# Two conditioned attention layers: VectorE's transpose for the next first film moves behind the keys' reciprocal

## The reference

```
# layer 0
xn = layer_norm(x) * w + b;  q, k, v = xn @ Wq + bq, xn @ Wk + bk, xn @ Wv + bv
y  = softmax_over_keys(q k^T + mask) v                  # per head, 256 x 256 scores
h  = (layer_norm(y) * w2 + b2) * (1 + scale) + shift
x  = x + silu(h) @ Wo + bo
# layer 1
xn = layer_norm(x);  q, k, v as above;  masked keys are -inf, masked values 0
q  = softmax(q) over the 16 features of a head;  k = softmax(k) over the 256 tokens
y  = q (k^T v)                                          # per head, 16 x 16
h  = layer_norm(y) * (1 + scale) + shift
out = x + silu(h) @ Wo + bo
```

## Time and profile before

| | |
|---|---|
| median of 3 runs | 873.64 us (873.52 to 874.52) |
| profiled execution | 874.82 us, span 873.0, mean granted clock 0.998 |
| PE busy, whole span | 837.5 us (96%) |
| PEld (weight loads) | 686.3 us (79%) |
| DVE | 772.4 us (88%) |
| ACT | 679.9 us (78%) |
| POOL | 678.8 us (78%) |
| chain that ended last, by engine | PE 74%, DVE 14%, issue 7% |

### The profile page before, as it was taken

The page is one execution under the profiler, slowest core; times in us unless marked ns, Lnnn a source line. Parts: engine busy times, 40 slices in busy tenths (PEclk is TensorE's granted clock), DMA queues, the critical chain, the costliest instruction groups (busy, mean ns, idle before and its releaser), DMA issues.

```text
span 873.0 us, 23658 instructions
## 1 busy us (share of the span) xinstructions
PE 837.5 (96%) x8092; PEld 686.3 (79%) x8092; DVE 772.4 (88%) x1590; ACT 679.9 (78%) x1208; POOL 678.8 (78%) x1165
## 2 busy tenths in 40 slices
PE   5899999999999999999999988999999999999996
PEld 5677777777777777777777557899999999999996
DVE  5789999999999999999988867899999999999976
ACT  2257777878777777777787895899999999999975
POOL 3467878788888888888876247888888888888875
PEclk9999999999999999999999999999999999999999
DMA  7865565656565555656553313344444444444301
GB/s 256 272 204 168 200 209 199 212 190 214 179 218 184 208 200 208 205 192 221 190 199 140 117 57 115 96 142 135 138 133 136 144 133 138 136 150 141 110 31 61
DMA packets 129847, 143.69 MB, mean 165 GB/s; under 512 B 13312, under 2 KB 85984, under 8 KB 129600
## 3 DMA queue, kind: packets, MB, share of 16 engines
q1 hardware_dynamic: 129728, 142.19, 49.8%
HBM read 49.50 MB, written 38.11 MB: 100 GB/s over the span
## 4 chain that ended last, share of the span: by engine, by line
PE 74%; DVE 14%; issue 7%; ACT 1%; POOL 1%; DMA 1%; SPq 1%; DVEq 0%; ACTq 0%; POOLq 0%
PE psY L1721 12%; PE psX L1600 11%; PE psT L1600 9%; PE psM L1600 9%; DVE sb_cm L1158 6%; PE psT L1700 5%; PE psY L1600 4%; PE psT L1679 4%; PE psT L1883 4%; PE psT L1611 3%; PE psY L1836 3%; PE psM L1700 3%; PE psY L1746 2%; DVE sb_xF L1172 2%; PE psM L1679 2%
## 5 line engine op out<-in xcount | busy, mean ns | idle before, releaser
L1158 DVE TENSOR_REDUCE sb_cm<-psT 128x4 f32<-128x1024 f32 x168 | 202.7, 1213 | 20.4 <-PE psT L1700 20.2
L741 ACT ACTIVATE sb_P<-psT 128x1024 f32<-128x1024 f32 x176 | 177.9, 1025 | 44.1 <-PE psY L1721 23.5
L1721 PE MATMUL psY<-sb_P,sb_Vp 128*17 128x256 f32 x2048 | 129.4, 381 | 1.9 <-DVE sb_yr L1193 1.4
L1158 DVE TENSOR_REDUCE sb_cm<-psM 128x4 f32<-128x1024 f32 x88 | 106.7, 1213 | 11.6 <-PE psM L1700 11.5
L741 ACT ACTIVATE sb_P<-psM 128x1024 f32<-128x1024 f32 x80 | 82.0, 1025 | 21.6 <-PE psY L1721 11.7
L1600 PE MATMUL psX<-sb_xT,sb_W0h 128*128 128x256 f32 x488 | 93.6, 294 | 0.0
L1721 PEld LDWEIGHTS psY<-sb_P,sb_Vp 128*17 128x17 f32 x2048 | 50.3, 97 | 46.9 <-DVE sb_yr L1193 1.9
L521 POOL TENSOR_TENSOR sb_qp<-sb_qp 128x512 fp32r<-128x512 f32 x64 | 82.3, 1286 | 5.3
L1700 PE MATMUL psT<-sb_Ks,sb_Qs 64*128 64x256 f32 x672 | 76.6, 310 | 3.0 <-DVE sb_cm L1158 1.9
L1679 PE MATMUL psT<-sb_Qs,sb_Ks 64*128 64x256 f32 x704 | 75.5, 298 | 1.6 <-ACT sb_P L741 1.4
L1600 PEld LDWEIGHTS psX<-sb_xT,sb_W0h 128*128 128x128 f32 x488 | 71.5, 192 | 4.6 <-ACT sb_qp L764 0.2
(11 more groups left out here) (215 smaller groups left out, 2549.5 us busy)
## 6 DMA issues: line engine op xcount, KB each, us to landing
sb_Qs<-sb_qp SPq DMA_DIRECT2D x96, 256.0 KB
sb_Ks<-sb_qp SPq DMA_DIRECT2D x96, 256.0 KB
sb_xt<-in_x SPq DMA_DIRECT2D x32, 256.0 KB, 3.5
y_normed<-sb_Yn SPq DMA_DIRECT2D x32, 256.0 KB, 3.1
sb_u<-y_normed SPq DMA_DIRECT2D x128, 64.0 KB, 2.6
out<-sb_v SPq DMA_DIRECT2D x31, 256.0 KB, 2.4
x_biased<-sb_xo SPq DMA_DIRECT2D x28, 256.0 KB, 2.3
sb_u<-x_biased SPq DMA_DIRECT2D x28, 256.0 KB, 3.4
```

Of the source, the lines that this page charges most:

```text
L741: a.activation(P[G % 4][:, :], pairs[place["S", n, g][0]][:, :], ACT.Exp).then_inc(s_ex, 1)
L1158: v.tensor_reduce(cm[n % 2][:, 4 * j:4 * j + 4], scores, AX.X, ALU.max, negate=True).then_inc(s_mx, 1)
L1721: ins = pe.matmul(psY[32 * j:32 * j + 17, y0:y0 + T], Vp[n % RING][:, m, 4 * gr + j, :], Pj[:, c0:c0 + 256], start=(m == 0), stop=(m == 1))
```

## The change

In VectorE's `second(t)` the call `yt_(t + 1)` moves from behind `h_(t - 5, 1)` to behind `kd_(t - 2)`, ahead of `yd_(t - 3)`. Nothing else changes, on no other engine.

```diff
@@ VectorE, second(t)
                 if ok(t - 5):
                     h_(t - 5, 1)
-                if ok(t + 1):
-                    yt_(t + 1)
                 if 0 <= t - 4 < BLOCKS:
                     ynt_(t - 4)
                 if ok(t - 2):
...
                     ob_(t - 6)
                 if ok(t - 2):
                     kd_(t - 2)
+                if ok(t + 1):
+                    yt_(t + 1)
                 if ok(t - 3):
                     yd_(t - 3)
```

## The result

The changed kernel took 869.26 us as the median of 11 runs (865.72 to 873.96), the kernel before 873.64 (11 runs, 872.29 to 876.40) on the same chip: ratio 0.9944 [0.9925, 0.9962]. In a second series of six runs an unchanged copy of it (experiment 1) took 868.49 against 875.25, ratio 0.9927 [0.9907, 0.9947]. The sign holds, and so does the mechanism, as the rest shows; the medians moved by 4.4 and 6.8 us where 8.1 was forecast. The 869.26 lies in the whole range (864.4 to 870.2) but outside the forecast's own (864.4 to 867). The profiled execution took 869.6 us, 5.2 less than the profiled one before.

The account below looks back on a forecast made before the run. A VectorE-TensorE loop through BD was taken to bound the turn, not TensorE's work. 25 stalls of 0.29 us (7.3) plus 0.9 for the first turns, 8.2 off, gave 865.5 us; own range 864.4 to 867, whole range 864.4 to 870.2.

Parts of the forecast that it names:

- A: Rival, chance 0.24: the loop through `kd_` becomes the bound, turns of 10.27 to 10.33 us, time 868.5 us.
- The BD loop and the 0.29: VectorE and TensorE wait for each other over BD and y products: 10.473 us against TensorE's 10.18, 0.29 a turn.
- What comes earlier: `ynt_` to `kd_` on VectorE can start up to 0.62 us earlier; BD margin 0.38, `ob_` waits for its product.
- What is queued behind: `yd_` and `xl_` now follow `yt_` on VectorE; `yd_` at most 0.13 us later, 1.37 behind the y load.
- the cover of the keys' load: Slack between the end of `xl_` on VectorE and TensorE's keys' weight load: 0.19 us left after the change.
- The next loop: Reciprocal, `xn_`, keys' sums, `kd_`, `yt_`: 10.13 to 10.19 us against TensorE's 10.18, so TensorE just becomes the bound.
- the reasoning about GpSimd: GpSimd's root would start some tenths earlier, before VectorE's two-input product; if caught, `xn_` comes 1.87 us after it, not 1.73.
- The sum: Second layer: 25 y products at 0.29 us, 7.3 us, plus 0.9 for the first turns, 8.2 us.
- the start: Turns 4 and 5, where VectorE's sequence paces: 0.26 and 0.62 us, together 0.9; bounds 0.3 to 2 us.
- From the sum to the time: Profiled 874.82 us less 8.2 gives 866.6; the runs' median 873.64 less 8.2 gives 865.4; stated as 865.5.
- B: Rival, chance 0.06: TensorE is saturated, its late y load is no lost time, nothing moves: 873.6 us.
- C: Rival, chance 0.04: ScalarE's late second film delays its sums, `kd_`, and now `yt_` and `yd_`: slower, 880 us.

Follow-up runs that it names:

- experiment 1: Unchanged copy of the changed kernel, run again beside the kernel before: 868.49 us (6 runs), ratio 0.9927 to the kernel before.
- Experiment 7: Kernel before, with one of the three terms of the keys' product on TensorE left out in turns 3 to 27: 876.65 us, ratio 1.0013 to the kernel before.
- experiments 3: Kernel before, with VectorE's transpose `yt_` moved only to right ahead of `bd_`: 875.88 us, ratio 1.0006 to the kernel before.
- experiment 4: Kernel before, with `yt_` moved to right behind `bd_`, ahead of `ob_`: 868.58 us, ratio 0.9918 to the kernel before.
- experiment 5: Kernel before, `yt_` in its old place but transposing only 32 of 512 columns from film 5 on: 870.17 us, ratio 0.9934 to the kernel before.
- experiment 9: Changed kernel, with `yt_` one call later, behind `yd_` and ahead of `xl_`: 877.10 us, ratio 1.0037 to the kernel before.
- experiment 6: Changed kernel, with one of the three terms of the keys' product left out in turns 3 to 27: 868.32 us, ratio 0.9907 to the kernel before.
- experiment 8: Kernel before, with `yt_` right behind `bd_` and one of three terms of the keys' product left out: 866.35 us, ratio 0.9888 to the kernel before.

## Why the prediction was right, and where its size was off

The mechanism was right, and the time fell into the range partly by luck. The first series' 869.26 is outside the forecast's own range and nearer to A's 868.5 than to 865.5; it is inside the whole range because that had to reach A. By the time alone one would have said A, and the traces refute A: the turns are 10.187, not 10.27 to 10.33.

*The BD loop and the 0.29.* Right. The wait is gone, the turn is TensorE's own, 10.187 against the 10.18 read from turn 31. Experiment 7 shows that before it was not TensorE's work, and experiments 3, 4 and 5 that it was the loop through BD with the transpose in it.

*What comes earlier.* Right: BD ends 0.39 before it is asked for (0.38 forecast); `ob_` waits 0.26 (0.32).

*What is queued behind.* Right in sign, and the bound was too wide: `yd_` stays at 1.24 behind the y load (up to 1.37 was allowed), and so the cover of the keys' load is about 0.3 (experiment 9), not 0.19.

*The next loop, and A.* The loop exists, and it takes 10.04 (experiment 6), not 10.13 to 10.19: 6.49 for the way to `xn_` in place of 6.57, and 0.09 for `kd_` in place of 0.11 to 0.17. It was the tightest point of the forecast, and it has 0.15 us to spare. Here the reasoning about GpSimd was half right. The root starts earlier, 4.64 us after the reciprocal instead of 4.84 (702.35 - 697.71, 725.32 - 720.48), and is never held up. But the small product behind it is, so `xn_` comes 1.88 after the root (704.23 - 702.35), the 1.87 that A feared. The turn that the prediction took for the undisturbed one, 1.73, had a slow product as well, 0.61 us at 726.10. The earlier start pays for the difference. The prediction also has no term for the loop through `vk_` (9.99, experiment 8), which stays under TensorE's turn too.

*The sum.* The 24 turns between the y loads of films 3 and 27 gave 6.86, 0.286 each, and the three up to film 3 0.86; together 7.7 instead of 8.2. The term that was too large is the start. Turns 4 and 5, put at 0.26 and 0.62, gave 0.22 and 0.40 (y loads of films 0, 1 and 2 now 9.59 and 10.02 apart, before 9.81 and 10.42). Why turn 5 gave less than the whole 0.62 stays open. Film 3's stall gave 0.24, and the 24 turns lack another 0.1.

*From the sum to the time.* This is the weakest step: "the median of the runs is 1.2 below the profiled one", and less 8.2 "that gives 865.4". It took the spread of three runs, 1 us, for the kernel's own. The 11 runs of either kernel spread over 4 and 8 us; where the clock is on record the times go with its mean (866.61 at 1.000, 870.96 at 0.994 to 0.996), and the median of 11 came out at 869.26. Only runs at an equal clock show the change itself, 6.7 us. The last microsecond between this and the 7.7 of the profiled second layer isn't settled; turns such as the one of 10.78 in experiment 1, at 0.6 each, are the part of it that a trace showed (its y loads 0 to 31 took 310.21 against 309.31).

*B* fell with experiment 7. *C* is real as a mechanism and cost 0.1 us in the one turn that showed it (experiment 1).

## What to carry to other kernels

Two engines that wait for each other once a turn are a loop; add up its legs, and compare the sum with a turn in which the engine that looks full had no wait. An instruction is worth moving when the move takes it out of that loop, wherever it lands, until it meets the next thing that is due: here the keys' load after one step more, its own reader after two. Before a gain under one per cent is read from medians, sort the runs of both kernels by their mean granted clock.

## What was not expected of the hardware

The same program was granted 1.2 GHz for 0 to 14 us of an execution, in its first 64 us or between 505 and 568 us, around the passage to the second layer, and in other executions not at all. The start took 58.37 to 60.00 us in the six traces without a dip there, 59.89 with one of 3.4 us (experiment 9), 61.64, 62.00 and 62.19 with 6.8 (experiments 3, 4 and 7), and 63.33 and 63.29 with 10 (the kernel after, experiment 5). The DMA queues were the busiest part of the stretch shown, 0.87 and 0.90.

In three of the twelve traces something can be seen ahead of the fall. In the kernel after:

```profile
18.52 2.27 DVE L1121 SCALAR_TENSOR_TENSOR sb_W0l<-sb_W,sb_col,sb_W0h 128x256 fp32r<-128x256 f32 x2
```

```profile
20.84 0.50 PE L1600 MATMUL psT<-sb_W0l,sb_xT 128*128 128x256 f32 x2 [2.78 <-DVE sb_W0l L1121]
```

VectorE's two products for the weights' low part took 2.27 us, where the kernel before needs 0.88 (start 18.60). GpSimd had started its scaling of q (L518, then L521) at 18.50 and was at it until 20.50; in the kernel before it started at 19.38, when VectorE's products were nearly done. TensorE waited 2.78 for the low part (0.59 before), was busy for 0.06 us between 18 and 20, and had a granted clock of 0.82 between 21 and 22 and 0.50 from 22 to 28. Experiment 5 and experiment 7, which has the order before, show the same: 2.32 and 2.23 us, a wait of 2.78, and 0.50 from 22 to 28. In the nine other traces the two products took 0.88 to 1.23, TensorE's wait was 1.60 at most, and the clock stayed at 1.00 up to 26 us. So 1.3 of the 4.12 us (20.84 - 19.53 for the same matmul) were gone before the clock fell, and all of it lies some 500 us ahead of the first instruction that the diff moves. For the other dips no trace shows what sets them off; that the wait caused this one rests on three traces and no experiment.

A small instruction can take much longer beside the wrong neighbour: in experiment 8 GpSimd's root took 0.71 us for one norm and 1.13 to 1.23 for the other in the same turn, where it met VectorE's products of two SBUF tiles. The second one of a turn:

```profile
739.45 1.18 POOL L595 TENSOR_TENSOR sb_rs<-sb_ve,sb_ph 128x2 f32<-128x2 f32 x1
```

The product started at 739.38. It is the behaviour of the earlier trace rows, here in each turn but one of those from 679 to 760.
